# Unread products in front of TensorE's waits, and another order of turns in a decoder kernel's middle stage

## The chip, the cores and the metric

The kernel runs on one core of one Trainium2 chip, in one launch. The metric is the device time of that launch in microseconds (us). The kernel before took 3580.44 us, the median of three runs (3580.33 to 3582.51 us). TensorE is called PE below, as in the profile; VectorE is DVE, ScalarE is ACT, GpSimd is POOL and SyncE is SP.

## The reference, cut to what matters

The input x is 16 sequences of 256 tokens with 128 features, in float32. Four decoder layers follow each other. Each has a self-attention or another mixing block, a cross-attention to a context of 64 tokens for each sequence, and a feed-forward block. Each of the twelve blocks is added to its input and normalised:

```python
x = _layernorm(x + _L0_attn_ref(x, ...))    # a log-space scan
x = _layernorm(x + _L0_xattn_ref(x, ctx_1024, ...))
x = _layernorm(x + _L0_ffn_ref(x, ...))     # int8-like quantised, with global scales
x = _layernorm(x + _L1_attn_ref(x, ...))    # attention in segments of 64, dilated neighbours
x = _layernorm(x + _L1_xattn_ref(x, ctx_1024, masks, ...))   # 16 heads of 64
x = _layernorm(x + _L1_ffn_ref(x, ...))     # 8 experts choose their tokens
x = _layernorm(x + _L2_attn_ref(x, ...))    # gated long convolution
# ... L2 cross-attention, L2 quantised product, L3 retention, L3 cross- and self-attention, L3 ternary network
```

A layer norm subtracts the mean over the 128 features and divides by the root of variance plus 1e-5. So each block waits for a chain of reductions before the next one can begin.

## The kernel before, in words

Activations stay in SBUF, feature by token, in groups of T = 512 tokens (2 sequences), so there are 8 groups. The program is a row of stages: a first stage (layer 0 without the end of its feed-forward), global scales of the quantised block, a middle stage (from the quantised down product to the router of the experts), the choice and the experts, a short end stage (the norm after the experts), the spectral convolution, and a last stage (the rest of layers 2 and 3).

**Lanes.** The first, the end and the last stage work on two groups at a time, as two lanes. Each lane has its own half of PSUM: four banks of 128x512. Each engine's program for a lane is a Python generator, and `weave` (L790) takes a step of one lane and a step of the other in turn. Every engine so gets one fixed order of instructions, and executes it in that order; where the next instruction waits for a semaphore, everything behind it on this engine waits too. The first and the last stage are loops of four iterations, each over two groups.

**The middle stage.** It has two programs instead of two equal lanes. "Near" is the segment attention (`LaneSegment`, L1020) with its norm. "Far" is the cross-attention with 16 heads (`LaneWide`, L1267), its norm and the router (`LaneGate`, L1463), and behind these the "lead": the quantised down product (`LaneDown`, L980) and its norm for a later group. In loop iteration `it` near works on group `it`, far on group `it - 1` and lead on group `it + 1`. The string `MIDDLE` says whose step comes next, "n" or "f", for all engines alike (`turns`, L809). The loop has 6 iterations (`middle`, L2907). One more turn with both near and far follows the loop, then far alone for the last group; before the loop near of group 0 runs with lead of group 1 in the order `MIDDLE_ALONE`.

Near's steps on PE are: start (projections); for each of the two sequences scores, peaks, turned, out, back; then for each sequence dil_scores, dil_peaks, dil_turned, dil_out, dil_sum; near z; the norm. "Peaks" waits for a maximum on DVE (L1239), "turned" for the queries with the maximum put in (L1191), "out" for the exponential on ACT (L1179), and "dil_sum" for the weighted parts on DVE (L1256). Far's steps are two for the queries, one for keys and values, one for products of values with output weights, scores0, scores1, then for each of four tiles first/second (transposes L1356) and out (L1361, L1363, with the scores of the tile after next), the norm in two steps (DVE's statistics; then the transposes), the router, an empty step, and lead in five steps.

**A norm.** `LaneNorm` (L864) does bn_stats (L880) and bn_aggr (L884) on DVE, eps and the power -1/2 on POOL (L895, L897), the scaling of four tiles on DVE (L888), four transposes on PE in two halves (L908) and two copies on ACT (L919). In its step on PE, `meanwhile` first issues any product that is ready, then PE waits for the scaled tiles.

Of the kernel before, what the change touches and what calls it, by code (L numbers as in the profile page):

```python
# [27 lines left out]
P = 128  # L28
# [776 lines left out]

MIDDLE = "nfnfnfnfnfnfnfnfnfnffnfnfnnffnnfnfnfnfnfnffnfnfn"
MIDDLE_ALONE = "nnnnf" * 6
# [56 lines left out]
class LaneNorm:  # L864
# [35 lines left out]
    def pe(self, pe, n, meanwhile=None):  # L900
        m, sg = self.lane, self.sig
        yield
        if meanwhile is not None:
            meanwhile()
        for (half, _, tiles), bank in zip(self.halves, (0, 1)):
            pe.wait_ge(*sg.done("dve", f"scaled{tiles[-1]}", n))
            for k, i in enumerate(tiles):
                mm = pe.transpose(m.bank[:, bank, k * P:(k + 1) * P], m.xs[:, i, :], m.ident)  # L908
            mm.then_inc(*sg.up("pe", half + "features"))
        yield  # L910
# [69 lines left out]
class LaneDown:  # L980
# [20 lines left out]
    def pe(self, pe, n):  # L1001
        m, sg = self.lane, self.sig
        yield
        pe.wait_ge(*sg.done("dve", "q3", n))
        for c in range(CH):
            r = min(P, INNER - c * P)
            mm = pe.matmul(m.bank[:, 0, :], m.whole[0:r, QG + c, :], m.whole_h[0:r, c, :], start=(c == 0), stop=(c == CH - 1))
        mm.then_inc(*sg.up("pe", "product"))
        yield
        pe.wait_ge(*sg.done("dve", "resid", n))  # L1010
        for i in range(NT):
            mm = pe.transpose(m.bank[:, 3, i * P:(i + 1) * P], m.sum[:, i * P:(i + 1) * P], m.ident)
        mm.then_inc(*sg.up("pe", "z"))
        yield
# [5 lines left out]
class LaneSegment:  # L1020
# [21 lines left out]
    def peaks(self, pe, step):  # L1042
# [4 lines left out]
        mm.then_inc(*self.sig.up("pe", step))  # L1047

    def pe(self, pe, n, x_ready):
        m, sg, w = self.lane, self.sig, self.w  # L1050
        bank = m.bank
        pe.wait_ge(*x_ready)
        pe.matmul(bank[:, 0, :], w["q"], m.xf[:, :], start=True, stop=True).then_inc(*sg.up("pe", "q"))
# [12 lines left out]
        yield  # L1066
        for b in range(G):
            if b:
                pe.wait_ge(*sg.done("dve", f"norm{b - 1}", n))
            else:  # L1070
                pe.wait_ge(*sg.done("act", "v1", n))
                pe.wait_ge(*sg.done("dve", f"vd{G - 1}", n))
                m.carry_product(pe, bank)
# [7 lines left out]
            mm.then_inc(*sg.up("pe", f"scores{b}"))  # L1081
            yield
            pe.wait_ge(*sg.done("dve", f"max1_{b}", n))
            self.peaks(pe, f"peaks{b}")
            yield
            pe.wait_ge(*sg.done("dve", f"query1_{b}", n))
            for p in range(2):
# [6 lines left out]
            mm.then_inc(*sg.up("pe", f"turned{b}"))  # L1094
            yield
            pe.wait_ge(*sg.done("act", f"exp{b}", n))
            for half in range(2):
# [6 lines left out]
            mm.then_inc(*sg.up("pe", f"out{b}"))  # L1104
            yield
            pe.wait_ge(*sg.done("act", f"copied{b}", n))
            for i in range(2):
# [4 lines left out]
            yield  # L1112
        for b in range(G):
            if b:
                pe.wait_ge(*sg.done("act", f"middle{b - 1}", n))
            else:
                pe.wait_ge(*sg.done("dve", f"norm{G - 1}", n))
            for i in range(2):
                for r in range(4):
                    rows = slice(32 * r, 32 * r + 32)  # L1120
                    mm = pe.matmul(bank[:, r, i * S:(i + 1) * S], m.qf[rows, (2 * b + i) * P:(2 * b + i + 1) * P],
                                   m.dilkeys[rows, b, :], start=True, stop=True)
            mm.then_inc(*sg.up("pe", f"dil_scores{b}"))
            yield
            pe.wait_ge(*sg.done("dve", f"dil_max1_{b}", n))
            self.peaks(pe, f"dil_peaks{b}")
            yield
            pe.wait_ge(*sg.done("dve", f"dil_query1_{b}", n))
            for p in range(2):
                for r in range(4):  # L1130
                    rows = slice(32 * r, 32 * r + 32)
                    mm = pe.matmul(bank[:, r, p * S:(p + 1) * S], m.dilkeys[rows, b, p * P:(p + 1) * P],
                                   m.query[rows, p, :], start=True, stop=True)
            mm.then_inc(*sg.up("pe", f"dil_turned{b}"))
            yield
            pe.wait_ge(*sg.done("act", f"dil_exp{b}", n))
            for i in range(2):
                for c in range(8):
                    mm = pe.matmul(bank[:, 2 * i + c // 4, c % 4 * self.BLOCK:(c % 4 + 1) * self.BLOCK],  # L1139
                                   m.weights[:, c * S + i * P:c * S + (i + 1) * P],  # L1140
                                   m.dilvals[:, b, c * self.BLOCK:(c + 1) * self.BLOCK], start=True, stop=True)
            mm.then_inc(*sg.up("pe", f"dil_out{b}"))
            yield
            pe.wait_ge(*sg.done("dve", f"dil_part3_{b}", n))
            for i in range(2):
                out = bank[:, 0, i * P:(i + 1) * P]
                pe.matmul(out, m.heads[:, 2 * b + i, :], m.ident, start=True, stop=False)
                for g in range(SEGS):
                    mm = pe.matmul(out, m.parts[:, i, g, :], m.ident, start=False, stop=(g == SEGS - 1))
            mm.then_inc(*sg.up("pe", f"dil_sum{b}"))  # L1150
            yield
        pe.wait_ge(*sg.done("act", f"middle{G - 1}", n))
        summed(pe, bank[:, 3, :], ((m.resid, m.ident), (m.af, w["o"]))).then_inc(*sg.up("pe", "z"))
# [113 lines left out]
class LaneWide:  # L1267
# [26 lines left out]
    def pe(self, pe, n, x_ready):  # L1294
        m, sg, w = self.lane, self.sig, self.w
        bank = m.bank
        pe.wait_ge(*x_ready)
# [41 lines left out]

        pe.wait_ge(*sg.done("act", "w01", n))  # L1340
        pe.wait_ge(*sg.done("dve", "w11", n))
        pe.wait_ge(*sg.done("pool", "kmask", n))
        scores(0)
        yield
        pe.wait_ge(*sg.done("dve", "sub0", n))
        scores(1)
        yield
        for u in range(NT):
            pe.wait_ge(*sg.done("dve", f"mul{u}", n))
            for half, name in enumerate(("first", "second")):  # L1350
# [7 lines left out]
            yield  # L1358
            pe.wait_ge(*sg.done("act", f"copy1_{u}", n))
            out = bank[:, 3, u * P:(u + 1) * P]  # L1360
            pe.matmul(out, m.resid[:, u * P:(u + 1) * P], m.ident, start=True, stop=False)  # L1361
# [3 lines left out]
            mm.then_inc(*sg.up("pe", f"out{u}"))  # L1365
            if u + 2 < NT:
                pe.wait_ge(*sg.done("dve", f"sub{u + 1}", n))
                scores(u + 2)
# [94 lines left out]
class LaneGate:  # L1463
# [8 lines left out]
    def pe(self, pe, n, x_ready):  # L1472
        m = self.lane
        pe.wait_ge(*x_ready)
        for i in range(NT):
# [868 lines left out]
def decoder(nc, dram, out):  # L2344

    with ExitStack() as ctx:
# [146 lines left out]

        m.carry, m.carry_product = carry, carry_product

        lanes = [Memory(), Memory()]
        for i, lane in enumerate(lanes):
            lane.bank, lane.maskrow = m.banks[i], maskrows[i]
            lane.ident, lane.half2, lane.ones3, lane.whole, lane.rotary = m.ident, m.half2, m.ones3, m.whole, m.rotary
# [39 lines left out]
        for i, lane in enumerate(starts):  # L2539
            lane.bank, lane.ident, lane.half2, lane.one = m.banks[i], m.ident, m.half2, m.one  # L2540
            lane.eps4, lane.minus_half, lane.carry = m.eps4, m.minus_half, carry
# [19 lines left out]
        for lane in starts:  # L2561
# [3 lines left out]
            lane.peaks = lane.peaks_all.rearrange("p (a i c) -> p a i c", a=2, i=2)  # L2565

        near, far = Memory(), Memory()
        for i, lane in enumerate((near, far)):
            lane.bank, lane.ident, lane.half2, lane.eps4, lane.minus_half = m.banks[i], m.ident, m.half2, m.eps4, m.minus_half
            lane.carry, lane.carry_product, lane.whole, lane.whole_h, lane.downscale = carry, carry_product, m.whole, m.whole_h, m.downscale[:, 0:1]  # L2570
        near.xf, near.xs, near.resid, near.qf, near.af, near.heads = m.xf, m.xs, m.resid, m.qf, m.af, m.heads
# [26 lines left out]
        far.gate, far.gsmall, far.big = m.gate, m.gsmall, 2.0 ** 100  # L2598
        lead = Memory()
        lead.bank, lead.ident, lead.eps4, lead.minus_half, lead.carry = far.bank, m.ident, m.eps4, m.minus_half, carry  # L2600
        lead.whole, lead.whole_h, lead.downscale, lead.sum = m.whole, m.whole_h, m.downscale[:, 0:1], turned_out[:, :]
# [749 lines left out]
```

## Time and profile before

| | |
|---|---|
| median of 3 runs | 3580.44 us |
| the profiled execution, its own time | 3578.87 us |
| its span, first to last instruction | 3577.1 us |
| mean granted TensorE clock | 0.828 of full speed |
| PE matmul busy | 2514.6 us, 70% of the span |
| DVE busy | 1733.8 us, 48% |
| ACT busy | 1030.3 us, 29% |
| POOL busy | 342.0 us, 10% |

Times inside the trace are counted from the first instruction. The busy time of PE is that of its matmul records. A float32 product with 128 columns shows as two records, a transpose as one. PEclk is the clock that the throttle granted to TensorE: 1.0 is 2.4 GHz and 0.5 is 1.2 GHz, and a value between them is a mixture over the stretch. In a row of the timeline, "[2.83 <-DVE spread L1256]" is the time for which the engine had been idle before the row, and what released it.

### The profile page before, as it was taken

The numbers are of one execution on the slowest core, as the hardware profiler recorded it, in microseconds if no ns is written. First come the engines' busy times: TensorE is split into PE (matmuls) and PEld (weight loads), VectorE is DVE, ScalarE is ACT, GpSimd is POOL, SyncE is SP. The second block draws the span as 40 slices with busy tenths as digits, with TensorE's granted clock in tenths as the row PEclk, the third lists the DMA queues.
The fourth block names the chain that finished last, engine by engine and source line by source line (L and its number), as shares of the span: only waits on it lengthen the run. The fifth ranks groups of instructions, "written<-read, shape, count | busy, mean of one in ns | idle before, by whom it ended". The sixth has DMA issues, their size and how long they took to land.

```text
span 3577.1 us, 50939 instructions
## 1 busy us (share of the span) xinstructions
PE 2514.6 (70%) x20374; PEld 1693.0 (47%) x20374; DVE 1733.8 (48%) x4213; ACT 1030.3 (29%) x1406; POOL 342.0 (10%) x580
## 2 busy tenths in 40 slices
PE   4555258778877887458567779677796777967778
PEld 3334146666656665335444444444444444444444
DVE  4555744556555553551347551475414754157541
ACT  3333412222222221011122343223422243222432
POOL 0100000000000000036201000110001100011000
PEclk8777558878887887678888899878997899987999
DMA  2000000000000000202710000000000000000000
GB/s 77 0 0 0 2 1 1 8 7 7 1 7 8 7 1 7 87 16 29 144 67 1 1 7 1 1 1 1 7 0 1 1 1 7 1 1 1 1 1 24
DMA packets 39342, 47.97 MB, mean 13 GB/s; under 512 B 7169, under 2 KB 36369, under 8 KB 38354
## 3 DMA queue, kind: packets, MB, share of 16 engines
q1 hardware_dynamic: 33490, 40.43, 3.9%
q0 software_dynamic: 5632, 4.33, 0.9%
q8 instruction: 172, 2.82, 0.3%
q14 instruction: 48, 0.39, 0.0%
HBM read 31.81 MB, written 12.91 MB: 13 GB/s over the span
## 4 chain that ended last, share of the span: by engine, by line
issue 50%; PE 29%; DVE 14%; POOL 4%; ACT 2%; DMA 1%; POOLq 0%; DVEq 0%; SPq 0%; ACTq 0%
PE banks L2298 6%; PE banks L859 5%; DVE weights L2019 2%; PE banks L2287 1%; PE banks L560 1%; PE banks L908 1%; PE banks L2222 1%; DVE xs L888 1%; POOL rstd L897 1%; PE banks L571 1%; PE banks L1918 1%; DVE dilvals L880 1%; PE banks L1139 1%; PE banks L762 1%; POOL dilvals L897 1%
## 5 line engine op out<-in xcount | busy, mean ns | idle before, releaser
L880 DVE BATCH_NORM_STATS2 stats<-banks 128x6 f32<-128x128 f32 x208 | 46.4, 285 | 337.5 <-PE banks L859 289.7
L2190 DVE TENSOR_REDUCE wide_area<-banks 128x8 f32<-128x2048 f32 x64 | 146.6, 2291 | 107.3 <-PE banks L2110 107.3
L2162 ACT ACTIVATE weights<-banks 128x2048 f32<-128x2048 f32 x64 | 120.1, 1877 | 121.5 <-PE banks L2123 121.5
L895 POOL TENSOR_TENSOR rstd<-moments,eps 128x4 f32<-128x4 f32 x56 | 11.2, 199 | 1429.5 <-DVE moments L884 1429.5
L908 PE MATMUL banks<-wA,xs 128*128 128x128 f32 x208 | 55.2, 368 | 110.5 <-DVE xs L888 110.0
L1683 DVE TENSOR_REDUCE wide_area<-banks 128x16 f32<-128x1024 f32 x80 | 94.1, 1218 | 58.6 <-PE banks L1596 58.6
L880 DVE BATCH_NORM_STATS2 dilvals<-banks 128x6 f32<-128x128 f32 x144 | 32.1, 285 | 183.8 <-PE banks L859 183.8
L1139 PE MATMUL banks<-wC,weights 128*128 128x72 f32 x512 | 90.0, 359 | 18.0 <-ACT weights L1179 18.0
L908 PE MATMUL banks<-wA,gates 128*128 128x128 f32 x144 | 36.7, 344 | 90.8 <-DVE gates L888 89.9
L1139 PEld LDWEIGHTS banks<-wC,weights 128*128 128x128 f32 x512 | 87.7, 271 | 24.5 <-ACT weights L1179 24.5
L888 DVE TENSOR_SCALAR xs<-banks,moments,rstd 128x128 f32<-128x128 f32 x208 | 71.0, 404 | 39.7 <-POOL rstd L897 38.7
L908 PEld LDWEIGHTS banks<-wA,xs 128*128 128x128 f32 x208 | 26.4, 171 | 134.4 <-DVE xs L888 132.0
L2298 PE MATMUL banks<-wide_area,big 128*128 128x512 f32 x192 | 86.3, 592 | 0.0
L1336 PE MATMUL banks<-gates,wide_area 128*128 128x128 f32 x512 | 86.0, 319 | 0.0
L919 ACT ACTIVATE xf<-banks 128x256 f32<-128x256 f32 x64 | 24.4, 383 | 194.8 <-PE banks L908 194.3
L1336 PEld LDWEIGHTS banks<-gates,wide_area 128*128 128x128 f32 x512 | 72.1, 218 | 16.7 <-issue 16.7
L895 POOL TENSOR_TENSOR smalls<-smalls,eps 128x4 f32<-128x4 f32 x16 | 3.2, 199 | 790.2 <-DVE smalls L884 790.2
L2019 DVE TENSOR_TENSOR weights<-banks,wC 128x2048 f32<-128x2048 f32 x32 | 72.1, 2284 | 12.8 <-PE banks L1907 12.8
L1649 ACT ACTIVATE weights<-banks 128x2048 f32<-128x2048 f32 x32 | 60.1, 1877 | 58.7 <-PE banks L1610 58.4
L1356 PE MATMUL banks<-wA,weights 128*128 128x128 f32 x256 | 45.1, 303 | 37.0 <-ACT spread L1403 30.8
L908 PEld LDWEIGHTS banks<-wA,gates 128*128 128x128 f32 x144 | 16.2, 157 | 111.8 <-DVE gates L888 111.8
L859 PE MATMUL banks<-wA,resid 128*128 128x128 f32 x288 | 62.4, 300 | 9.1 <-DVE wide_area L1548 6.0
(744 smaller groups left out, 6424.7 us busy)
## 6 DMA issues: line engine op xcount, KB each, us to landing
big<-in_wE SPq DMA_DIRECT2D x1, 4096.0 KB, 13.1
weights<-long_kernel SPq DMA_DIRECT2D x8, 512.0 KB, 7.4
conv<-wide_area SPq DMA_DIRECT2D x16, 256.0 KB, 2.7
wC<-in_wC SPq DMA_DIRECT2D x1, 3012.0 KB, 16.7
wC<-in_wG SPq DMA_DIRECT2D x1, 2971.0 KB, 19.3
big<-in_wT SPq DMA_DIRECT2D x1, 2560.0 KB, 11.6
x_all<-in_xT SPq DMA_DIRECT2D x1, 2048.0 KB, 10.4
rows<-spread SPq DMA_DIRECT2D x8, 256.0 KB, 3.1
```

The source lines that it names most:

```text
L859: mm = pe.matmul(bank[:, i * P:(i + 1) * P], left[:, i * P:(i + 1) * P], right, start=(k == 0), stop=(k == len(terms) - 1))
L880: dve.bn_stats(m.stats[:, i, :], self.tokens(i)).then_inc(*sg.up("dve", f"stats{i}"))
L888: dve.tensor_scalar(m.xs[:, i, :], self.tokens(i), m.moments[:, i, 0:1], m.rstd[:, i:i + 1], ALU.subtract, ALU.mult).then_inc(*sg.up("dve" ...
L897: pool.tensor_tensor(m.rstd, m.rstd, m.minus_half[:, :], ALU.pow).then_inc(*sg.up("pool", "rstd"))
L908: mm = pe.transpose(m.bank[:, bank, k * P:(k + 1) * P], m.xs[:, i, :], m.ident)
L1139: mm = pe.matmul(bank[:, 2 * i + c // 4, c % 4 * self.BLOCK:(c % 4 + 1) * self.BLOCK], m.weights[:, c * S + i * P:c * S + (i + 1) * P], m. ...
L1336: mm = pe.matmul(bank[:, i, (p % 4) * P:(p % 4 + 1) * P], m.wide_q[:, p, u * P:(u + 1) * P], m.wide_k[:, p, u // 2, :, :].rearrange("p j k ...
L1683: dve.tensor_reduce(m.peaks[:, p, :, :].rearrange("p i (r c) -> p r i c", r=4)[:, :, :, at:at + 2], bank[:, :, :].rearrange("p r (i j k) - ...
L2019: dve.tensor_tensor(m.weights.rearrange("p (h q) -> p h q", h=H), bank[:, :, :].rearrange("p r (j q) -> p (r j) q", j=4), m.causal[:, 0:P] ...
L2162: act.activation(m.weights, bank[:, :, :].rearrange("p r c -> p (r c)"), ACT.Exp, scale=DK ** -0.5)\
L2190: dve.tensor_reduce(m.peaks[:, k % 2, :, :].rearrange("p t (r c) -> p r t c", r=4)[:, :, :, SPARE[j]], bank[:, :, :].rearrange("p r (t k) ...
L2298: mm = pe.matmul(m.bank[:, c, :], w[name][:, k * FF + c * P:k * FF + (c + 1) * P], src[k], start=(k == 0), stop=(k == FC - 1))
```

## The change

Three things change.

A helper issues products of the identity with itself (128x128 by 128x128, float32) into columns 0 to 127 of a bank that holds nothing of use at that point. Nobody reads them and they signal nothing. `BUSY` says how many stand at which place; a place without an entry has none:

```diff
+BUSY = {'first1': 2, 'dil_sum0': 7, 'wide scores1': 8, 'lead norm': 10, 'near norm': 1, 'dil_peaks1': 12, 'dil_peaks0': 2, 'lead product': 5, 'wide start': 2, 'gate': 7, 'back0': 3, 'first3': 1, 'first0': 1, 'last norm': 8, 'first norm': 6}
...
+        def keep_busy(pe, bank, place):
+            for _ in range(BUSY.get(place, 0)):
+                pe.matmul(bank[:, 0:P], m.ident, m.ident, start=True, stop=True)
```

They are issued on PE right before a wait. The name of a norm is that of its lane: "first" for the two lanes of the first stage, "last" for the lanes of the end stage and of the last stage, "near", "far" and "lead" in the middle:

```diff
@@ LaneNorm.pe
         if meanwhile is not None:
             meanwhile()
+        m.keep_busy(pe, m.bank[:, 1, :], m.name + " norm")
         for (half, _, tiles), bank in zip(self.halves, (0, 1)):
             pe.wait_ge(*sg.done("dve", f"scaled{tiles[-1]}", n))
@@ LaneDown.pe
+        if not (isinstance(n, int) and n == 0):
+            m.keep_busy(pe, m.bank[:, 1, :], "lead product")
         pe.wait_ge(*sg.done("dve", "q3", n))
@@ LaneSegment
+    def pause(self, pe, place):
+        if self.lane.beside["free"]:
+            self.lane.keep_busy(pe, self.lane.beside["bank"], place)
...
+            self.pause(pe, f"back{b}")
             pe.wait_ge(*sg.done("act", f"copied{b}", n))
...
+            self.pause(pe, f"dil_peaks{b}")
             pe.wait_ge(*sg.done("dve", f"dil_max1_{b}", n))
...
+            self.pause(pe, f"dil_sum{b}")
             pe.wait_ge(*sg.done("dve", f"dil_part3_{b}", n))
@@ LaneWide.pe
+        beside["free"], beside["bank"] = False, bank[:, 2, :]
+        m.keep_busy(pe, bank[:, 1, :], "wide start")
         pe.wait_ge(*x_ready)
...
         pe.wait_ge(*sg.done("act", "w01", n))
+        beside["free"] = True
...
+        m.keep_busy(pe, bank[:, 2, :], "wide scores1")
         pe.wait_ge(*sg.done("dve", "sub0", n))
...
         for u in range(NT):
+            m.keep_busy(pe, bank[:, 2, :], f"first{u}")
+            beside["free"] = False
             pe.wait_ge(*sg.done("dve", f"mul{u}", n))
...
             pe.wait_ge(*sg.done("act", f"copy1_{u}", n))
+            beside["free"] = True
@@ LaneGate.pe
+        m.keep_busy(pe, m.bank[:, 2, :], "gate")
+        m.beside["free"] = False
         pe.wait_ge(*x_ready)
```

Near has no bank to spare and uses bank 2 of far, and only where far doesn't need it. The flag `beside["free"]` is a Python value, read while the program is written out, so it depends on the order of turns.

The order of turns is the third part:

```diff
-MIDDLE = "nfnfnfnfnfnfnfnfnfnffnfnfnnffnnfnfnfnfnfnffnfnfn"
+MIDDLE = "nfnfnfnfnfnfnfnfnfnffnfnfnnfnnfnnnffffnfnffnffnn"
```

Up to near's dil_turned0 and far's last out the two strings agree. Behind that:

```
before: far norm (statistics), near dil_out0, near dil_sum0, far norm (transposes), near dil_scores1, router,
        near dil_peaks1, (empty), near dil_turned1, lead quantisation, near dil_out1, lead product, near dil_sum1, ...
after:  near dil_out0, near dil_sum0, far norm (statistics), near dil_scores1, near dil_peaks1, near dil_turned1,
        far norm (transposes), router, (empty), lead quantisation, near dil_out1, lead product, near dil_sum1, ...
```

The rest is the same again (lead z, lead norm, near z, the transposes of the lead norm and of the near norm).

## Rows read from the trace of the kernel before

**Rows 1.** Busy time by stage (start:end, length, busy us of each engine, PEclk, DMA)

```profile
45.00:400.00 355.00, 200.55 (x1365) 130.65 (x1363) 192.54 (x490) 132.61 (x175) 33.78 (x76) 0.75 0.00 1
540.00:1457.00 917.00, 723.41 (x6609) 568.70 (x6610) 476.88 (x888) 219.72 (x320) 49.04 (x110) 0.81 0.02 5
1808.00:3577.00 1769.00, 1312.90 (x9998) 803.68 (x9998) 836.87 (x2104) 575.98 (x768) 145.76 (x265) 0.89 0.01 5
```

**Rows 2.** PE's waits at norms, last stage (total us, times, longest)

```profile
PE banks L908 <- DVE gates L888: 81.3, 50, 3.5
PE banks L908 <- DVE xs L888: 70.1, 34, 3.3
```

**Rows 3.** Two norms in PE's timeline, last stage

```profile
2598.24 0.95 PE L908 MATMUL banks<-wA,xs 128*128 128x128 f32 x4 [1.89 <-DVE xs L888]
...
2671.54 0.60 PE L908 MATMUL banks<-wA,xs 128*128 128x128 f32 x4
```

**Rows 4.** Busy time behind norm waits, first and last of twelve; the whole iteration

```profile
2248.00:2256.00 8.00, 4.15 (x6) 1.44 (x6) 0.14 (x1) 3.19 (x5) 1.64 (x6) 0.57 0.02 5
...
2599.00:2604.00 5.00, 4.53 (x8) 1.84 (x7) 1.36 (x4) 2.42 (x4) 0.07 (x1) 0.66 0.00 0
2248.00:2688.00 440.00, 328.63 (x2498) 200.19 (x2498) 208.72 (x526) 144.12 (x192) 36.38 (x66) 0.89 0.01 2
```

**Rows 5.** The same work in two iterations of the last stage

```profile
2247.55:2307.65 60.10, 39.36 (x313) 24.00 (x313) 28.07 (x78) 22.12 (x27) 7.95 (x21) 0.86 0.01 2
2688.04:2749.91 61.87, 40.31 (x312) 25.61 (x312) 28.04 (x78) 22.02 (x27) 7.95 (x21) 0.83 0.01 2
```

**Rows 6.** Two iterations of the middle stage's loop

```profile
917.10:1033.10 116.00, 91.86 (x893) 72.49 (x891) 63.28 (x119) 28.60 (x42) 6.08 (x15) 0.84 0.02 6
...
1152.60:1275.50 122.90, 98.87 (x895) 77.45 (x895) 64.51 (x123) 29.20 (x43) 7.14 (x17) 0.78 0.02 6
```

**Rows 7.** The price of 128-column records at full and at half clock

```profile
2660.37 4.46 PE banks L859 x40
...
881.37 1.92 PE L1149 MATMUL banks<-wA,spread 128*128 128x128 f32 x8
```

**Rows 8.** Three slow stretches in one iteration of the middle loop

```profile
835.00:846.00 11.00, 10.31 (x71) 7.66 (x70) 8.19 (x9) 2.23 (x4) 0.00 (x0) 0.53 0.01 1
879.00:887.00 8.00, 6.21 (x36) 5.84 (x40) 2.97 (x9) 1.24 (x4) 0.00 (x0) 0.57 0.25 68
889.00:911.00 22.00, 16.54 (x79) 13.86 (x79) 9.48 (x19) 2.57 (x4) 1.60 (x5) 0.53 0.01 1
```

**Rows 9.** PE's waits, middle stage

```profile
PE banks L1332 <- DVE weights L1440: 17.6, 8, 2.6
```

**Rows 10.** PE's timeline, the end of one middle iteration

```profile
874.21 3.75 PE L1139 MATMUL banks<-wC,weights 128*128 128x72 f32 x32
880.79 0.79 PE L1147 MATMUL banks<-wA,heads 128*128 128x128 f32 x2 [2.83 <-DVE spread L1256]
...
887.33 1.06 PE L1476 MATMUL banks<-wC,spread 128*128 128x8 f32 x8
889.88 1.12 PE L1046 MATMUL banks<-wA,spread 128*128 128x128 f32 x4 [1.50 <-DVE spread L1239]
...
896.05 7.10 PE L1139 MATMUL banks<-wC,weights 128*128 128x72 f32 x32 [2.00 <-ACT weights L1179]
...
915.28 0.44 PE L908 MATMUL banks<-wA,big 128*128 128x128 f32 x2 [2.02 <-DVE big L888]
```

**Rows 11.** DVE and ACT beside it

```profile
887.47 2.35 DVE L1239 TENSOR_REDUCE spread<-banks 128x64 f32<-128x1024 f32 x2 [5.47 <-PE banks L1121]
...
885.97 0.72 ACT L919 ACTIVATE spread<-banks 128x256 f32<-128x256 f32 x2
```

**Rows 12.** PE's waits, first stage

```profile
PE banks L859 <- DVE big L1774: 38.1, 3, 12.7
```

**Rows 13.** A norm in PE's timeline, end stage

```profile
1750.12 0.44 PE L908 MATMUL banks<-wA,xs 128*128 128x128 f32 x2 [0.61 <-DVE xs L888]
```

More of the change, by code:

```diff
@@ L1009, in pe @@
         yield
+        m.keep_busy(pe, m.bank[:, 1, :], "lead z")
         pe.wait_ge(*sg.done("dve", "resid", n))
@@ L1051, in pe @@
         bank = m.bank
+        m.keep_busy(pe, bank[:, 1, :], "near start")
         pe.wait_ge(*x_ready)
@@ L1067, in pe @@
         for b in range(G):
+            self.pause(pe, f"scores{b}")
             if b:
@@ L1082, in pe @@
             yield
+            self.pause(pe, f"peaks{b}")
             pe.wait_ge(*sg.done("dve", f"max1_{b}", n))
@@ L1085, in pe @@
             yield
+            self.pause(pe, f"turned{b}")
             pe.wait_ge(*sg.done("dve", f"query1_{b}", n))
@@ L1095, in pe @@
             yield
+            self.pause(pe, f"out{b}")
             pe.wait_ge(*sg.done("act", f"exp{b}", n))
@@ L1113, in pe @@
         for b in range(G):
+            self.pause(pe, f"dil_scores{b}")
             if b:
@@ L1127, in pe @@
             yield
+            self.pause(pe, f"dil_turned{b}")
             pe.wait_ge(*sg.done("dve", f"dil_query1_{b}", n))
@@ L1135, in pe @@
             yield
+            self.pause(pe, f"dil_out{b}")
             pe.wait_ge(*sg.done("act", f"dil_exp{b}", n))
@@ L1151, in pe @@
             yield
+        self.pause(pe, "near z")
         pe.wait_ge(*sg.done("act", f"middle{G - 1}", n))
@@ L1295, in pe @@
         m, sg, w = self.lane, self.sig, self.w
-        bank = m.bank
+        bank, beside = m.bank, m.beside
+        beside["free"], beside["bank"] = False, bank[:, 2, :]
+        m.keep_busy(pe, bank[:, 1, :], "wide start")
         pe.wait_ge(*x_ready)
@@ L1340, in pe @@
         pe.wait_ge(*sg.done("act", "w01", n))
+        beside["free"] = True
+        m.keep_busy(pe, bank[:, 2, :], "wide scores0")
         pe.wait_ge(*sg.done("dve", "w11", n))
@@ L1366, in pe @@
             if u + 2 < NT:
+                m.keep_busy(pe, bank[:, 2, :], f"wide scores{u + 2}")
                 pe.wait_ge(*sg.done("dve", f"sub{u + 1}", n))
@@ L2492, in carry_product @@
             pe.matmul(banks[:, 0, 0:1], m.ident, m.ident[:, 0:1], start=True, stop=True)
-        m.carry, m.carry_product = carry, carry_product
+        def keep_busy(pe, bank, place):
+            for _ in range(BUSY.get(place, 0)):
+                pe.matmul(bank[:, 0:P], m.ident, m.ident, start=True, stop=True)
+        m.carry, m.carry_product, m.keep_busy = carry, carry_product, keep_busy
         lanes = [Memory(), Memory()]
         for i, lane in enumerate(lanes):
-            lane.bank, lane.maskrow = m.banks[i], maskrows[i]
+            lane.bank, lane.maskrow, lane.keep_busy, lane.name = m.banks[i], maskrows[i], keep_busy, "last"
             lane.ident, lane.half2, lane.ones3, lane.whole, lane.rotary = m.ident, m.half2, m.ones3, m.whole, m.rotary
@@ L2539, in decoder @@
         for i, lane in enumerate(starts):
-            lane.bank, lane.ident, lane.half2, lane.one = m.banks[i], m.ident, m.half2, m.one
+            lane.bank, lane.ident, lane.half2, lane.one, lane.keep_busy, lane.name = m.banks[i], m.ident, m.half2, m.one, keep_busy, "first"
             lane.eps4, lane.minus_half, lane.carry = m.eps4, m.minus_half, carry
@@ L2565, in decoder @@
             lane.peaks = lane.peaks_all.rearrange("p (a i c) -> p a i c", a=2, i=2)
+        beside = {"free": False}
         near, far = Memory(), Memory()
@@ L2569, in decoder @@
             lane.bank, lane.ident, lane.half2, lane.eps4, lane.minus_half = m.banks[i], m.ident, m.half2, m.eps4, m.minus_half
+            lane.keep_busy, lane.name, lane.beside = keep_busy, ("near", "far")[i], beside
             lane.carry, lane.carry_product, lane.whole, lane.whole_h, lane.downscale = carry, carry_product, m.whole, m.whole_h, m.downscale[:, 0:1]
@@ L2599, in decoder @@
         lead = Memory()
+        lead.keep_busy, lead.name = keep_busy, "lead"
         lead.bank, lead.ident, lead.eps4, lead.minus_half, lead.carry = far.bank, m.ident, m.eps4, m.minus_half, carry
```

## The prediction

> **What bounds the kernel now.** I first read the busy table by stage, with the granted clock beside it. PE is the busiest engine of every stretch listed, at 56% of the first stage, 79% of the middle and 74% of the last; DVE follows at 54%, 52% and 47% [rows 1]. So no engine is full, and each stage is a chain in which PE's work alternates with waits. The reader is to see the clock: 0.75, 0.81 and 0.89. A clock c over t us means that 2(1 - c)t us ran at 1.2 GHz: 177 us, 348 us and 389 us, 914 us together. (The chain of waits that ended last follows POOL here, which idles most of the time, and says little; I did not use it.)
>
> Then the waits of PE. In the last stage it waits 151 us at the transposes of norms in 84 pieces [rows 2], and behind such waits the clock falls. I read the clock behind every norm of one iteration (2248 to 2688 us): it is low behind twelve. The first of these stretches has 0.57 over 8 us and the last 0.66 over 5 us [rows 4], 6.9 and 3.4 us at half clock; the twelve sum to 68 us, of 97 us in the iteration (0.89 over 440).
>
> What a slow microsecond costs is to be had from equal work done twice. The same 60 us of the last stage took 60.10 us at 0.86 and 61.87 at 0.83 [rows 5]: 16.8 against 21.0 us slow, 1.77 us longer, 0.42 us for each. Two iterations of the middle loop took 116.0 us at 0.84 and 122.9 at 0.78 [rows 6]: 37.1 against 54.1 us, again 0.41. With nothing else on the path it would be 0.5. So I take 0.42 everywhere: slow time stands mostly where PE is the path.
>
> **The price of one product.** Forty records of 128 float32 columns took 4.46 us at full clock, so a product, which is two records, takes 0.223 us; eight took 1.92 us at half clock, so a product there costs up to 0.48 us [rows 7]. I take 0.22 and 0.45. The change issues 96 in the first stage (16 norms of 6), 445 in the middle, 64 in the end stage and 512 in the last: 1117, or 249 us of PE at full clock. Nearly all of it must lie in waits, or the kernel gets slower.
>
> **Last stage: 16 norms in each of four iterations, 8 products each.** Eight take 1.8 us at full clock. Thirteen norms of an iteration have a wait, the shortest of 1.89 us [rows 3]; there the products cost nothing. The other three find their tiles ready, as the one at 2671.54, which stands inside unbroken PE work [rows 3]: 3 x 1.8 = 5.4 us. I add 0.5 us for products that run slow in a short wait. Gain: between nothing and all 68 us of slow time. The products fill 1.8 of 1.9 to 3.5 us [rows 2, 3], so part of a long wait stays idle, and the 29 us behind other waits stay as they are. I take 37 of the 68: 37 x 0.42 = 15.5. Net 9.6 us, for four iterations 38.
>
> A rule of the Trainium skill bears on this: "TensorE: Matmul & The Clock Gate", Part 1 (The HAM clock gate), has the gate drop the clock only after an idle stretch without work, so one product anywhere in a wait of this size would hold it. The trace does not agree: the norm with only 1.89 us of wait, with work before and behind it, is followed by a slow stretch [rows 3, 4].
>
> **Middle stage: seven turns with near and far.** One iteration has three slow stretches: 0.53 over 11 us from 835 us, 0.57 over 8 us from 879, 0.53 over 22 us from 889 [rows 8], so 10.3 + 6.9 + 20.7 = 37.9 us. In front of them stand PE's waits for far's first softmax (17.6 us in eight, so 2.2 each) [rows 9], for near's weighted parts (2.83) and for near's maxima (1.50) [rows 10]. "wide scores1" puts 8 products (1.8 us) into the first, "dil_sum0" 7 (1.6) into the second and "dil_peaks1" 12 (2.7) into the third. I take 25 of the 37.9, two thirds, since the fills match the waits better here: 25 x 0.42 = 10.5 us. The ends are 0 and 37.9 (15.9 us).
>
> Against it stand these costs of a turn:
> - The order. Before, the router's product hid in the wait for near's maxima, beside 2.35 us on DVE [rows 10, 11]. Now far's norm transposes come behind near's dil_turned1, and the router needs the copies of them by ACT. ACT is then in near's exponential (PE waited 2.00 us for it [rows 10]) and copies after it, 0.72 us for the two halves [rows 11]. Dil_out1 stands behind the router on PE: it starts later by these copies, some 0.2 us of handing over and the router's eight records (0.9 us at full clock, 1.06 at half [rows 10]). That is 1.8 us. It can be less only if PE reaches the router late. In return the four transposes leave the path (4 x 0.11 = 0.45). The 7 products of "gate" (1.6 us) lie in the wait for the exponential. Net 1.35.
> - "dil_peaks1": 2.7 us in a wait that is now about 2.5 long, since the router has left it: 0.2. "lead norm": 10 products, 2.2 us, in a wait of 2.02 [rows 10]: 0.2. "back0" and "wide scores1" follow each other, 11 products in one wait of 2.2: 0.25.
> - "wide start": no wait, 2 products, 0.45. "first0", "first1" and "first3" and "near norm": 5 products, half hidden: 0.5. "lead product", 5 products (1.1 us), is hidden while DVE forms near's last parts. "dil_peaks0" issues nothing: far's first3 has just set the flag to false.
>
> These sum to 2.95 us. Net 10.5 - 2.95 = 7.5 us a turn, 53 for seven. The statistics of far's norm come later on DVE, but into a place where DVE waits for PE.
>
> **First and end stage.** In the first stage much of the slow time follows DVE's scan (PE waits 12.7 us for it [rows 12]), which no product fills. I take a fifth of the 177 us, 35: 35 x 0.42 = 15 us, less 2 for products in its shorter waits, 13. The ends are a loss of 4 (all products slow) and twice 13. In the end stage half of the eight norms wait about 0.6 us [rows 13]: 1.8 - 0.6 = 1.2 us too much, less what the other lane takes up; I take 3 us lost, between 0 and 5.
>
> **Sum.** -38 - 53 - 13 + 3 = -101 us against the profiled execution's own 3578.87 us (span 3577.1, 1.8 us around it): 3478. The median shown is 1.6 us above this execution, which is within the rounding of my terms. Forecast 3479 us.
>
> **The rivals.**
> - Less is held (A). The falls only move to the next wait. My gains are 62, 74 and 15 us, 151 together, and my costs 24, 21, 2 and 3, 50 together. Half of the gain is 75, which leaves 25: 3554; two thirds leave 51: 3528. For it: the loop's turn, retention's waits and the scan get no product. Against it: the products stand at the twelve places where I saw falls.
> - More is held (B), every slow stretch listed: last 68 x 0.42 - 5.9 = 22.7 us, x 4 = 91; middle 15.9 - 3 = 12.9, x 7 = 91; first 26: about 3374. This is also what the skill's rule above would give. Against it: the row that contradicts the rule, and fills that end well before the longest waits (3.5 us) do.
> - Slower (C). The clock stays low at the products, and they run at 0.45 us. Eight are then 3.6 us, and in the last stage 1.89 to 3.5 us of wait no longer hold them: about 10 us of overrun in thirteen waits and 3 x 3.6 in the rest, 21 an iteration, 84 in all; the middle loses some 9 us a turn, 63; the first and end stage 10. With no clock gained that is 3736; with a fifth of the 914 slow us regained (77 us) about 3659. It decides from the point where the slow time regained times 0.42 is less than the costs: 119 us of it with products at full clock (50 us), more the slower they run. For it: a clock that is low takes long solid work to rise (the 22 us stretch was 75% busy [rows 8]). Against it: most norm waits begin at full clock.
> - The order (D). The router's detour alone: 1.35 x 7 = 9 us lost, and in the new order the near chain of the second sequence is not held at full clock: the middle gains 10 instead of 53, 3522. It falls beside A.
>
> **How the numbers follow.** Forecast (3440 to 3515) 0.55; A and D (3515 to 3572) 0.22; B (below 3440) 0.11; no change 0.04; C 0.08. The range must leave out at most two in ten: I cut most of B and of C, 3420 to 3560. Of a change, about 0.2% (7 us) can be told from none: faster 0.88, same 0.04, slower 0.08.
>
> **What would show it.** The granted clock of the last stage goes from 0.89 to about 0.93, of the middle from 0.81 to about 0.9, of the first from 0.75 to 0.79. An iteration of the last stage takes about 430.5 us instead of 440, one of the middle about 111 instead of 116 to 123. The waits at L908 shrink by nearly the 1.8 us of products before them. Near's second dil_out takes 3.75 us instead of 7.10 [rows 10], but starts nearly 2 us after the exponential ends. The forecast is wrong in its gain if the clocks are as before, and wrong in its costs if the clocks rise and the iterations don't shorten.

## The result, and the profile after

The kernel after takes 3458.41 us, the median of four runs (3451.88 to 3460.84), against 3580.39 for the kernel before (four runs). The ratio is 0.9657, with a 95% interval of 0.964 to 0.9673. That is 122 us less; the forecast was 3479, 101 us less.

The same stages, between the same instructions, in the profile after. The columns are those of [rows 1]: start and end, length, busy us of each engine with its instructions, PEclk, DMA. First the first stage, then middle and last stage, then one iteration of the last stage's loop:

```profile
40.00:361.40 321.40, 208.46 (x1541) 148.70 (x1541) 173.35 (x440) 116.66 (x155) 32.39 (x74) 0.81 0.00 1
456.50:1393.40 936.90, 782.78 (x8003) 637.75 (x8003) 506.90 (x946) 232.18 (x335) 51.29 (x116) 0.91 0.02 6
1734.60:3451.30 1716.70, 1348.30 (x11024) 882.42 (x11024) 837.31 (x2104) 573.90 (x767) 145.67 (x264) 0.95 0.01 4
2165.00:2595.00 430.00, 337.79 (x2756) 221.72 (x2756) 209.34 (x526) 143.36 (x193) 36.33 (x67) 0.94 0.01 2
```

And between the same instructions in the kernel before:

```profile
40.00:368.10 328.10, 192.87 (x1349) 129.08 (x1350) 173.16 (x440) 117.00 (x155) 32.39 (x74) 0.76 0.00 1
463.10:1463.50 1000.40, 774.57 (x7134) 606.84 (x7134) 506.47 (x947) 232.45 (x335) 51.30 (x116) 0.79 0.02 5
1805.50:3569.80 1764.30, 1314.02 (x10000) 803.98 (x10000) 836.87 (x2104) 575.60 (x767) 145.57 (x264) 0.89 0.01 4
```

The reader is to see that DVE, ACT and POOL do the same busy time, and that PE has more records yet hardly more busy time, since its own work runs faster at the higher clock (0.91 against 0.79 in the middle). The middle is 63.5 us shorter, the last stage 47.6 and the first 6.7. PE's waits at the norms of the last stage shrink from 151 us [rows 2] to 59:

```profile
PE banks L911 <- DVE gates L890: 30.6, 52, 1.7
PE banks L911 <- DVE xs L890: 28.2, 40, 1.5
```

The end of a middle turn, which answers to [rows 10, 11], with its products (L2530, two records each), in order of start:

```profile
850.90 1.77 PE L2530 MATMUL banks<-wA 128*128 128x128 f32 x14
853.89 0.49 PE L1169 MATMUL banks<-wA,heads 128*128 128x128 f32 x2 [1.22 <-DVE spread L1279]
...
858.18 2.94 PE L2530 MATMUL banks<-wA 128*128 128x128 f32 x24
860.97 0.60 PE L1052 MATMUL banks<-wA,spread 128*128 128x128 f32 x4
...
863.75 1.88 ACT L1202 ACTIVATE weights<-banks 128x2048 f32<-128x2048 f32 x1 [6.69 <-PE banks L1152]
864.10 1.73 PE L2530 MATMUL banks<-wA 128*128 128x128 f32 x14
865.52 0.66 ACT L922 ACTIVATE spread<-banks 128x256 f32<-128x256 f32 x2
866.23 1.06 PE L1510 MATMUL banks<-wC,spread 128*128 128x8 f32 x8 [0.40 <-ACT spread L922]
867.14 5.72 PE L1160 MATMUL banks<-wC,weights 128*128 128x72 f32 x32
...
880.83 2.40 PE L2530 MATMUL banks<-wA 128*128 128x128 f32 x20
```

The wait for the weighted parts, 2.83 us, is now products for most of it and 1.22 us idle. The twelve products before dil_peaks1 fill its wait to the end. The router's detour is there as forecast: the exponential ends at 865.63, dil_out1 starts at 867.14, 1.5 us later. Dil_out1 begins at full clock and the clock falls within it, to a mean of 0.64:

```profile
867.00:873.00 6.00, 6.00 (x37) 6.00 (x37) 4.72 (x9) 0.23 (x1) 1.60 (x5) 0.64 0.05 5
```

In the seven turns with near and far it takes 3.77 us four times, and 5.18, 5.72 and 5.44 us in the others; before it took 7.10 in each.

### The profile page after: what moved, and what is told of

Read it like the earlier page. It is cut to its first block, busy times and chain, and to the rows that moved or that the text cites. A ratio compares the mean times of both kernels' runs of the same rounds, so it can differ in the third digit from the quotient of the medians.

```text
span 3458.5 us, 55406 instructions
## 1 busy us (share of the span) xinstructions
PE 2590.2 (75%) x22608; PEld 1840.1 (53%) x22608; DVE 1735.0 (50%) x4213; ACT 1027.3 (30%) x1406; POOL 342.1 (10%) x580
## 4 chain that ended last, share of the span: by engine, by line
issue 49%; PE 29%; DVE 14%; POOL 4%; ACT 2%; DMA 1%; SPq 0%; POOLq 0%; DVEq 0%; ACTq 0%
PE banks L2332 6%; PE banks L861 5%; DVE weights L2053 2%; PE banks L2530 2%; PE banks L560 1%; PE banks L2321 1%; DVE xs L890 1%; PE banks L571 1%; PE banks L1952 1%; PE banks L2256 1%; PE banks L911 1%; POOL rstd L899 1%; PE banks L762 1%; DVE dilvals L882 1%; PE banks L1160 1%
## 5 line engine op out<-in xcount | busy, mean ns | idle before, releaser
L2530 PE MATMUL banks<-wA 128*128 128x128 f32 x2234 | 303.5, 289 | 0.0
L2530 PEld LDWEIGHTS banks<-wA 128*128 128x128 f32 x2234 | 284.7, 204 | 15.0 <-issue 14.0
L911 PE MATMUL banks<-wA,xs 128*128 128x128 f32 x208 | 43.9, 303 | 52.9 <-DVE xs L890 52.2
L1160 PE MATMUL banks<-wC,weights 128*128 128x72 f32 x512 | 71.7, 308 | 4.1 <-ACT weights L1202 4.1
L1361 PE MATMUL banks<-gates,wide_area 128*128 128x128 f32 x512 | 74.1, 288 | 0.0
L1160 PEld LDWEIGHTS banks<-wC,weights 128*128 128x128 f32 x512 | 69.8, 222 | 5.5 <-ACT weights L1202 5.5
L861 PE MATMUL banks<-wA,big 128*128 128x128 f32 x128 | 29.5, 423 | 54.2 <-DVE big L1808 50.8
L1361 PEld LDWEIGHTS banks<-gates,wide_area 128*128 128x128 f32 x512 | 61.9, 191 | 14.5 <-issue 14.5
L1386 PE MATMUL banks<-wA,weights 128*128 128x128 f32 x256 | 40.9, 283 | 31.3 <-ACT spread L1435 27.3
```

The costliest lines, as they stand in the source:

```text
L861: mm = pe.matmul(bank[:, i * P:(i + 1) * P], left[:, i * P:(i + 1) * P], right, start=(k == 0), stop=(k == len(terms) - 1))
L1361: mm = pe.matmul(bank[:, i, (p % 4) * P:(p % 4 + 1) * P], m.wide_q[:, p, u * P:(u + 1) * P], m.wide_k[:, p, u // 2, :, :].rearrange("p j k ...
L2530: pe.matmul(bank[:, 0:P], m.ident, m.ident, start=True, stop=True)
```

## The experiments

Twelve kernels ran beside the kernel before, the order alone ten times and each of the others four times. The table gives each profile by stage: length, and behind the stroke the slow time in it, that is the us at 1.2 GHz, summed over stretches of 1 us as 2(1 - PEclk). The lengths run between the same instructions in each profile. What lies between the stages, 435 to 439 us with the end stage, is alike in all. The time is the median of a kernel's runs, the stages are those of one of them, which can lie 10 us away: for "order only" it is the fastest of ten (3570.5), for "four at last norms" the fastest (3478.1) and for "one product each" the slowest (3563.8).

```
kernel                  time us  ratio (95%)              first     middle     last
before                  3580.4                            328/157   1000/416   1764/389
after (the change)      3458.4   0.9657 (0.9640-0.9673)   321/123    937/159   1717/184
order only              3580.2   1.0009 (0.9995-1.0023)   321/137   1001/392   1761/386
old order, products     3457.9   0.9659 (0.9643-0.9675)   321/122    939/209   1719/195
last norms only         3529.3   0.9864 (0.9847-0.9882)   321/136   1002/416   1720/184
one column              3627.7   1.0133 (1.0113-1.0153)   329/157   1030/444   1787/422
one product each        3556.4   0.9929 (0.9908-0.9950)   321/137    999/402   1755/365
four at last norms      3486.1   0.9747 (0.9731-0.9764)   319/118    939/164   1736/277
ready norms without     3438.5   0.9614 (0.9598-0.9630)   319/121    938/168   1697/174
moved                   3421.9   0.9567 (0.9551-0.9584)   321/126    936/163   1680/106
before the turn         3442.3   0.9616 (0.9600-0.9632)   320/118    937/125   1705/143
moved and turn          3417.9   0.9538 (0.9522-0.9554)   318/117    932/134   1684/102
first norms without     3467.2   0.9670 (0.9653-0.9686)   327/152    938/162   1719/195
three middle places     3503.2   0.9778 (0.9762-0.9794)   319/118    979/317   1715/184
```

### Parts of the change

**Order only.** `BUSY = {}`, the new `MIDDLE`.

> Only the new order of turns, no products at all. My theory: the order by itself costs, since the router's detour puts copies and the router in front of near's second dil_out, 1.35 us a turn (1.8 less the transposes that leave the path), seven turns: about +9 us, 3588 to 3592, and the granted clock stays at 0.83. Rival: the order brings part of the gain itself (a norm wait that disappears, 2 us a turn): 3560 to 3570. Second rival: the clock moves either way by which wait falls where, within 20 us.

Measured 1.0009, no difference from before, and in the profile a middle of the same length. The detour is in the trace: the exponential ends at 888.54 and dil_out1 starts at 890.05, as in the change.

```profile
886.66 1.88 ACT L1202 ACTIVATE weights<-banks 128x2048 f32<-128x2048 f32 x1 [7.39 <-PE banks L1152]
888.43 0.65 ACT L922 ACTIVATE spread<-banks 128x256 f32<-128x256 f32 x2
889.14 1.06 PE L1510 MATMUL banks<-wC,spread 128*128 128x8 f32 x8 [1.48 <-ACT spread L922]
890.05 5.78 PE L1160 MATMUL banks<-wC,weights 128*128 128x72 f32 x32
```

The middle had 24 us less of slow time, which at the price found below is worth 8 us; that this hides the 9 us of the detour fits, but is argued. This profile is also the fastest of ten runs, 10 us below their median, so its stages can't settle a cost of 9 us; the interval (0.9995 to 1.0023, at most 8 us lost) can. The 9 us did not show.

**Old order, with the products.** The old `MIDDLE`, everything else as in the change.

> All products, the order of before. In this order the flag is false at near's dil_peaks1, so its 12 products are not issued. Theory: first and last stage keep their full gain (7 and 48 us), the middle keeps the two other places and loses the third, about 30 of its 63 us: near 3490. Rival, the order is only a cost: 3440 to 3455, faster than the change.

Both were wrong: 3457.9, the same as the change to 0.5 us. The middle has 50 us more of slow time, which goes with the absence of dil_peaks1's 12 products, and is only 2 us longer. So the new order buys nothing that shows: what it allows to hold, it seems to lose by the detour and the 12 products.

**Last norms only.** The old order, `BUSY = {'last norm': 8}`.

> Old order, products only at the norms of the end and the last stage (8 each). Theory: the parts are independent, the gain is that of the last stage in the traces, 48 us: 3532. Rival, the stages' gains depend on each other through where the loops start: off by more than 10 us. In the middle the granted clock stays at 0.81.

Measured 3529.3 against 3532 expected, and a last stage of 1720 us, as in the change; the middle is as before (1002 us). The parts add up stage by stage.

### What a product costs, and what holds the clock

**One column.** The moving operand is cut, the count is kept:

```diff
-pe.matmul(bank[:, 0:P], m.ident, m.ident, start=True, stop=True)
+pe.matmul(bank[:, 0:1], m.ident, m.ident[:, 0:1], start=True, stop=True)
```

> As the change, the same count of products at the same places, but each reads one column of the identity instead of 128, so it writes one column. Theory (what holds the clock is how much TensorE does in a wait): little is held, the granted clock stays near 0.84 to 0.86 and the time is 3540 to 3580. Rival (any product in a wait holds it, as the clock gate's rule reads): the clock is 0.89 or above and, since these products take a quarter of the time, 3420 to 3445.

Neither: it is slower than before, by 1.33%. The trace says why. Eight products before a norm of the last stage, first with one column, then in the change with 128:

```profile
2199.05 1.84 PE L2530 MATMUL banks<-wA 128*128 128x1 f32 x16
2201.95 0.95 PE L911 MATMUL banks<-wA,gates 128*128 128x128 f32 x4 [1.06 <-DVE gates L890]
```

```profile
2574.25 1.95 PE L2530 MATMUL banks<-wA 128*128 128x128 f32 x16
2576.04 0.60 PE L911 MATMUL banks<-wA,xs 128*128 128x128 f32 x4
```

They take the same time, 0.11 us a record. The likely reason is that each record also loads 128 columns of weights: the load records are alike in both runs, first with one column (with its matmul records below it), then in the change:

```profile
L2530 PEld LDWEIGHTS banks<-wA x2234: 186/192/338, 48.7 to 3619.6; 128*128 128x128 f32 x187
L2530 PE MATMUL banks<-wA x2234: 167/250/373, 48.8 to 3619.7; 128*128 128x1 f32 x187
L2530 PEld LDWEIGHTS banks<-wA x2234: 186/192/338, 48.2 to 3448.1; 128*128 128x128 f32 x187
```

(durations in ns, minimum/median/maximum; one load starts before the last has ended, which is how records of 192 ns follow each other every 112). So this run has the change's delays and not its clock, and separates the two. The delays cost 48 us in all by the medians; in the profiles it is 30 in the middle, 23 in the last stage and 1 in the first. A part of that, which this run doesn't separate, is slow time again: 28 and 33 us more of it than before. The columns, at no cost in time, bring 169 us: 3627.7 to 3458.4. The weight loads without the columns held nothing; the rule of the Trainium skill as the prediction read it ("TensorE: Matmul & The Clock Gate", Part 1), by which any product would do, does not describe this kernel.

From here comes the price of slow time. Last stage: 1787.3 to 1716.7 us, 70.6 us for 238 us of slow time less, 0.30 each. Middle: 1030.4 to 936.9, 93.5 for 285, 0.33. The same two stages of the run with one column (first busy time and records: PE), to be held against the rows of the change above, show what makes up this price:

```profile
463.80:1494.20 1030.40, 885.36 (x7997) 729.20 (x8004) 507.81 (x947) 232.51 (x335) 51.29 (x116) 0.78 0.02 5
1835.80:3623.10 1787.30, 1434.74 (x11024) 931.13 (x11024) 835.60 (x2104) 576.46 (x767) 145.41 (x264) 0.88 0.01 4
```

With the columns PE's busy time falls by 102.6 us in the middle and by 86.4 in the last stage, 0.36 for each slow microsecond in both, and not 0.5. The rest of the difference is idle time of PE, which grows by 9 us in the middle and by 16 in the last stage.

**One product each.** All entries of `BUSY` set to 1.

> As the change, but one product of 128 columns at each place instead of up to 12. Theory (the amount of work in a wait decides): costs fall to about 6 us and little is held, 3565 to 3585, clock 0.83. Rival (a product anywhere in a wait holds the clock): costs of 6 us with the whole gain of the clock, 3400 to 3420.

Measured 3556.4, 9 us below the expected range and 21 us below before, of which 9 in the last stage, where the slow time falls by 24 us of 389. The rival is excluded: a single product holds a small part.

**Four at the last norms.** `'last norm': 4`.

> As the change, with 4 products instead of 8 at each norm of the end and the last stage. Theory (the amount of work in a wait decides, and half of it holds about half): the three ready norms cost 2.7 us less an iteration (11 in all), but the last stage's slow time goes from 184 back to about 280 us, 29 us at 0.30: near 3476. Rival (4 are enough): 3447.

Measured 3486.1, as expected but for 10 us; the slow time is 277 us, as expected to 3, in a profile that is 8 us below the median. With 0, 1, 4 and 8 products at the norms it is 389, 365, 277 and 184 us: 23 to 29 us for each product. Among these four counts there is no step at which "enough" begins.

### Which places matter

**First norms without.** `'first norm'` left out of `BUSY`.

> As the change, without the 6 products at the norms of the first stage. The forecast had put 13 us of gain there. A run with no products at all and one with products only in the last stage had the same first stage as the change (321 us to the first transposes of the weights, against 328 in the profile of before). Theory: these products give nothing, 3455 to 3461. Rival (the forecast's term): 3471.

Measured 3467.2, 9 us above the change, in ratios 0.9670 against 0.9657 with overlapping intervals. That lies between the two expectations. In profiles the first stage is 327 to 329 us in three runs without these 128-column products (before, this one, and one column) and 321 in two others without them; with them, one or six, it is 318 to 321 in nine. So they give somewhere between nothing and 8 us. That is not settled.

**Three middle places.** `BUSY` with dil_sum0, dil_peaks1, wide scores1 and the norms of the other stages.

> As the change, with products in the middle stage only at near's dil_sum0 and dil_peaks1 and at wide scores1, the three places on which the forecast rests, and with the norms of the other stages. Left out: lead norm, lead product, gate, back0, wide start, near norm, first0, 1 and 3. Theory (those hold little and cost some 1.4 us a turn): 3445 to 3460. Rival (the lead norm's and the gate's products hold the clock through the end of the turn): 3475 to 3490, with the middle's slow time above 200 us.

My theory was wrong and the rival right in kind: 3503.2, 45 us above the change and 13 above the rival's range, with 317 us of slow time in the middle. The slow stretches in the trace point at two places above all. The clock falls at the router, where PE now waits 1.96 us for ACT without "gate"'s products, and again at the lead norm:

```profile
879.08 1.06 PE L1510 MATMUL banks<-wC,spread 128*128 128x8 f32 x8 [1.96 <-ACT spread L922]
879.99 7.07 PE L1160 MATMUL banks<-wC,weights 128*128 128x72 f32 x32
...
898.96 0.44 PE L911 MATMUL banks<-wA,big 128*128 128x128 f32 x2 [2.02 <-DVE big L890]
```

```profile
784.00:795.00 11.00, 7.17 (x48) 3.88 (x48) 3.01 (x7) 1.96 (x5) 1.04 (x2) 0.53 0.01 3
852.00:860.00 8.00, 6.77 (x40) 5.33 (x40) 1.57 (x3) 2.47 (x2) 0.00 (x0) 0.57 0.01 2
880.00:894.00 14.00, 12.45 (x57) 11.27 (x57) 7.94 (x15) 0.23 (x1) 1.60 (x5) 0.51 0.02 1
```

The second fence is the busy time of three stretches of this run: behind a lead norm, behind far's transposes L1386 (with waits of 0.65 and 0.69 us in front), and behind a router, with clocks of 0.53, 0.57 and 0.51. They are 10, 7 and 14 us slow. So dil_out1 takes 7.07 us, nearly the 7.10 of before. No run leaves out one of these places alone; what each is worth in time is not shown.

### Better versions

**Ready norms without.** No products at the three norms of an iteration whose tiles are ready.

```diff
+        if not getattr(self, "ready", False):
             m.keep_busy(pe, m.bank[:, 1, :], m.name + " norm")
...
+            g.norm[2].ready = True
+            g.norm[8].ready = lane is lanes[0]
```

> As the change, but without the 8 products at the three norms of a last-stage iteration whose tiles are ready (the norm behind the quantised product in both lanes, the last norm of the first lane). Theory: there the products are pure cost, 8 x 0.223 x 3 = 5.4 us an iteration, 21 us in all: 3437, with the slow time of the last stage as in the change (184 us). Rival: they also hold the clock for what follows, and the time comes back as slow time: 3450 to 3460.

Measured 3438.5: 19.9 us gained, the last stage 20 us shorter, its slow time not longer. The term of 5.4 us an iteration for these three norms is confirmed (5.0).

**Moved.** Beside that, products before the waits of the quantised product and of retention (how many, behind the #):

```diff
+        m.keep_busy(pe, m.bank[:, 2, :], "quant x")      # 12
         pe.wait_ge(*sg.done("dve", "whole", n))
...
+        m.keep_busy(pe, bank[:, 3, :], "turned")         # 8
         for i in range(NT):
             pe.wait_ge(*sg.done("dve", f"norm{i}", n))
```

> As the run without products at ready norms, plus 12 products before the wait for the quantised tokens (PE idles 4.6 and 2.4 us there) and 8 before the wait for retention's normed tiles (3.3 us). Theory: the slow time behind these waits, some 17 us of the 47 in an iteration, goes, at 0.30 us each: 5 us an iteration, 20 in all, on top of the 21: 3417. Rival (the falls move to retention's short waits behind): 3430 to 3440.

Measured 3421.9, as expected to 5 us. The last stage's slow time fell from 174 to 106 us.

**Before the turn.** Twelve products as the last thing in both loops' bodies.

```diff
                 turns(near(engine, it), both(far(engine, it - 1), lead(engine, it + 1)), MIDDLE)
+                if lead is lead_pe:
+                    keep_busy(engine, m.banks[0][:, 2, :], "turn")
...
                 weave(lane_pe(pe, 0, it), lane_pe(pe, 1, it), ticks)
+                keep_busy(pe, lanes[1].bank[:, 2, :], "turn")
```

> As the change, plus 12 products (2.7 us) as the last thing in the body of the middle's and of the last stage's loop, before the loop's turn, behind which PE stands idle 3.2 to 3.7 us. Theory: PE's sequencer takes the branch while the array still works on them, so they cost nothing and fill the idle time; the 10 us slow of a last-stage iteration and about 5 of a middle one go: (4 x 10 + 6 x 5) x 0.3 = 21 us, 3437. Rival: the turn begins only when the products are done: 2.7 us more in ten turns, 3460 to 3485.

Measured 3442.3, 16 us gained, where 21 were expected. The turn of the last stage's loop, in this run and in the change ("issue" is idle time in which PE waits for no semaphore that the profile shows):

```profile
2162.02 0.44 PE L911 MATMUL banks<-wA,gates 128*128 128x128 f32 x2 [0.20 <-DVE gates L890]
2162.29 2.84 PE L2530 MATMUL banks<-wA 128*128 128x128 f32 x24
2167.20 2.07 PE L1561 MATMUL banks<-x_all,wC 128*128 x2 [2.07 <-issue]
```

```profile
2163.05 0.44 PE L911 MATMUL banks<-wA,gates 128*128 128x128 f32 x2 [0.20 <-DVE gates L890]
2167.00 2.07 PE L1561 MATMUL banks<-x_all,wC 128*128 x2 [3.51 <-issue]
```

From the norm's last transposes to the next iteration's first product it is 5.2 us against 4.0: the 2.8 us of products lie over the turn for 1.6 of them, and the rest is paid. So they do not cost nothing, as the theory had it, but the clock makes up for it: 143 us of slow time in the last stage instead of 184, 125 in the middle instead of 159.

**Moved and turn**, both together:

> The two improvements together: products moved to waits in the last stage, and 12 before each loop's turn. Theory (the gains add, since they concern other stretches): 36 us from the first, 16 from the second, 3458 - 52 = 3406. Rival (the moved products already regain part of what the turn loses): 3412 to 3420.

3417.9 us, 0.9538 (0.9522 to 0.9554), the lowest median of all, 41 us below the change. The rival was right: the gains don't add, and the ratio's interval touches that of "moved" alone (0.9551 to 0.9584). Here the last stage was 1684 us, no shorter than with "moved" alone (1680); the middle was shorter by 4.

## Why the prediction was right or wrong

- **What bounds the kernel.** Right. The clock was the cause of the gain: with the delays and without the columns the kernel is slower than before, and the columns by themselves bring 169 us.
- **The price of a product.** 0.223 us at full clock, right (1.95 us for sixteen records). The expectation that one column would take a quarter of this was wrong.
- **The costs.** Right in sum, 50 us forecast and 48 measured with one column; in the profiles it is 23 in the last stage (forecast 24) and 30 in the middle (21). How much of this is delay alone stays open: by the prices of 0.30 and 0.33, 10 and 9 us of it are the added slow time. The three ready norms were 20 us, forecast 22. The detour of the router has the length forecast (1.5 us from the exponential's end, forecast 1.8), but no cost showed by itself. The 3 us lost in the end stage did not show either: what lies between the stages took 436.3 us, and 437.1 before. That the two lanes took them up is not shown.
- **Slow time regained.** Too low. In the last stage 205 us (389 to 184) against 4 x 37 = 148; in the middle 257 (416 to 159) against 7 x 25 = 175. I rested the middle on three places; the other places together are worth 45 us, and by the trace most of that stands at the lead norm and the router, which I booked as a cost of 0.2 us and as a free fill.
- **The price of slow time.** Too high. The term of 0.42 came from two pairs of stretches [rows 5, 6]; between runs that differ in hundreds of slow us it is 0.30 to 0.33. The pairs could not carry the term. A clock of two digits leaves each slow time of the last stage's pair uncertain by 0.6 us (0.005 x 2 x 60), so that 1.77 us for 4.2 us of slow time allows 0.33 to 0.59. The pair of the middle was not equal work: it holds 119 and 123 instructions of DVE. From the first product of an iteration to its last transposes, with 120 in both, it is 5.5 us for 13.7 us of slow time, 0.40, with 0.34 to 0.48 allowed in the same way:

```profile
921.10:1034.90 113.80, 92.34 (x893) 72.78 (x893) 63.98 (x120) 28.63 (x42) 6.70 (x15) 0.84 0.02 6
1157.30:1276.60 119.30, 98.36 (x893) 77.16 (x893) 63.99 (x120) 28.69 (x42) 6.70 (x15) 0.79 0.02 6
```

- **How the sum came out.** Too little slow time regained and too high a price for it went against each other, so that the forecast is nearer than its terms: that is luck. Against the run with one column (238 and 285 us of slow time less) the gain is 71 us in the last stage (forecast 62) and 94 in the middle (74), less the 23 and 30 us above: 48 and 64 net, against 38 and 53. These two stages are 20 us short. The first stage gave 6 less than forecast, the stretch between the stages 4 more, and 3 are the difference between profiles (118.6 us) and medians (122.0): together the 21 us by which the forecast was short.
- **First stage.** The term of 13 us was mis-sized. The profiles differ by 6.7, and two kernels without any product there show the same 321 us.
- **What would show it.** An iteration of the last stage: 430.5 forecast, 430.0 measured; one of the middle: 111, and 110.7 as the median of its six (before, between the same instructions, 117.9 to 119.6). The clocks: 0.93, 0.9 and 0.79 forecast, 0.95, 0.91 and 0.81 measured. Dil_out1 took 3.77 us in four of the seven turns (3.75 forecast); in the one shown it took 5.72, because the clock falls within it.
- **The rivals.** Less is held (A) and slower (C) did not come. What C describes, delays with no clock regained, is the run with one column, and it costs 48 us there, not the 80 to 156 of C. B did not come either: 184 us of slow time were left in the last stage. That any product would hold the clock was excluded by the one-column run and the run with one product each. D, the order as a loss, cannot be told from nothing.

## What to carry to other kernels

Where an engine's clock depends on its own work, put unread products of full width in front of its waits, no longer than the wait or only little longer (12 before the loops' turns overran by 1.2 us and still gained), and none where the operands are ready; read the clock behind each wait to find the places, small ones too, since a fall behind one wait slows everything up to the next rise. Before crediting such a change, run it once with the same instructions doing less, to separate what the instructions delay from what the clock gives back. Take the price of slow time from whole stages in runs that differ much in it: pairs of stretches that lay 4 and 17 slow us apart gave a third too much.

## What the runs showed of the hardware

A float32 product of 128x128 with one column took as long as one with 128, 0.22 us at full clock, but only with the second did the granted clock rise (0.823 with one column, 0.828 before, 0.894 with 128, over the whole kernel). The slow time of the last stage fell nearly evenly with the number of products at its norms: 389, 365, 277 and 184 us with 0, 1, 4 and 8. A microsecond at 1.2 GHz cost 0.30 to 0.33 us in stages where PE was busy 79 to 86% of the time. Products issued ahead of a loop's turn overlapped with its idle time in part, 1.6 of 2.8 us. And the new order, with a real detour of 1.5 us in seven turns, made no difference that shows.
